# Reciprocal denominators by way of device memory and DMA broadcast, in place of selector products on TensorE

## The reference

```
q = elu(t @ wq.T + bq) + 1 ;  k = elu(t @ wk.T + bk) + 1 ;  v = t @ wv.T + bv      # t: layer-normed tokens
q_cos, q_sin = q * cos, q * sin ; k_cos, k_sin = k * cos, k * sin                  # by token position
kv_cos, kv_sin = sum over tokens of k_cos (x) v, k_sin (x) v                       # 32 x 32 per head
qkv   = q_cos @ kv_cos + q_sin @ kv_sin
denom = 1 / (q_cos . sum(k_cos) + q_sin . sum(k_sin) + 1e-5)                       # one number per token and head
out   = (qkv * denom) joined over heads @ dense_w.T + dense_b                      # added to the stream
```

## Time and profile before

| | us |
|---|---|
| median of 3 runs | 2821.83 |
| the runs | 2802.16, 2821.9, 2821.83 |
| span of the profiled execution, first to last instruction | 2819.6 |
| TensorE / VectorE / ScalarE / GpSimd busy in it | 2421.4 / 2342.6 / 1724.8 / 1866.9 |

### The profile page before, as it was taken

One profiled execution on the slowest core, in us unless ns is written; L12 is line 12 of the kernel. 1 busy time (PEld: TensorE's weight loads), 2 busy tenths in 40 slices (PEclk: granted clock), 3 DMA queues, 4 the chain that ended last, 5 costly groups with the idle time before them and its releaser, 6 DMA issues.

```text
span 2819.6 us, 56945 instructions
## 1 busy us (share of the span) xinstructions
PE 2421.4 (86%) x19300; PEld 1207.1 (43%) x19300; DVE 2342.6 (83%) x3041; ACT 1724.8 (61%) x2821; POOL 1866.9 (66%) x1479
## 2 busy tenths in 40 slices
PE   3379999898989999898999989899998989999872
PEld 3324444444444444444444444444444444444442
DVE  4457999898988889898898989888898988899873
ACT  0057766666666666666666666666666666666640
POOL 0124677777767667776776777676677767777677
PEclk7579999999999999999999999999999999999995
DMA  9100000000000000000000000000000100000000
GB/s 249 35 10 10 10 16 16 16 6 12 16 17 16 16 16 11 7 16 17 16 16 16 14 4 16 17 16 16 17 15 2 16 17 16 16 10 7 7 7 12
DMA packets 232233, 55.14 MB, mean 20 GB/s; under 512 B 226065, under 2 KB 226945, under 8 KB 231777
## 3 DMA queue, kind: packets, MB, share of 16 engines
q1 hardware_dynamic: 231904, 50.95, 9.1%
HBM read 31.19 MB, written 12.85 MB: 16 GB/s over the span
## 4 chain that ended last, share of the span: by engine, by line
PE 40%; DVE 22%; POOL 17%; issue 14%; ACT 3%; DMA 1%; SPq 1%; POOLq 0%; DVEq 0%; ACTq 0%
PE ps L585 10%; PE ps L576 5%; PE ps L610 5%; DVE kbuf L994 5%; POOL prod L844 5%; DVE qbuf L1000 5%; PE ps L627 4%; PE ps L636 3%; POOL prod L847 3%; DVE rs L1017 2%; DVE route L1064 2%; POOL rstd L793 2%; PE ps L601 2%; ACT ebuf L716 2%; PE ps L568 2%
## 5 line engine op out<-in xcount | busy, mean ns | idle before, releaser
L716 ACT ACTIVATE ebuf<-ps,small 112x1024 f32<-112x1024 f32 x448 | 498.6, 1113 | 384.7 <-PE ps L576 357.3
L994 DVE SCALAR_TENSOR_TENSOR kbuf<-ps,ebuf 112x1024 f32<-112x1024 f32 x448 | 546.8, 1221 | 129.4 <-ACT ebuf L716 112.0
L721 ACT ACTIVATE ebuf<-ps,small 128x896 f32<-128x896 f32 x448 | 450.1, 1005 | 317.7 <-PE ps L601 237.8
L815 POOL TENSOR_TENSOR qbuf<-spread_r,qbuf 128x896 f32<-128x896 f32 x224 | 468.2, 2090 | 141.0 <-ACT spread_r L751 140.8
L585 PE MATMUL ps<-kbuf,xcs 112*64 112x512 f32 x1792 | 506.3, 651 | 45.1 <-DVE kbuf L994 45.1
L1000 DVE SCALAR_TENSOR_TENSOR qbuf<-ps,ebuf 128x896 f32<-128x896 f32 x448 | 486.3, 1085 | 37.6 <-ACT ebuf L721 35.3
L793 POOL TENSOR_TENSOR rstd<-varr,power 112x28 f32<-112x28 f32 x64 | 307.2, 4801 | 292.7 <-DVE varr L984 290.7
L636 PE MATMUL ps<-qbuf,gmat 128*64 128x224 f32 x3584 | 403.2, 369 | 4.5 <-DVE pbuf L1028 1.7
L844 POOL TENSOR_TENSOR prod<-prod 112x512 f32<-112x512 f32 x224 | 285.3, 1274 | 159.0 <-DVE prod L1084 157.9
L1084 DVE TENSOR_TENSOR prod<-ps,gate 112x1024 f32<-112x1024 f32 x224 | 272.4, 1217 | 94.4 <-PE ps L661 79.9
L627 PE MATMUL ps<-rs,sel 128*128 128x448 f16 x896 | 249.4, 360 | 96.6 <-issue 81.7
(11 more groups left out here) (133 smaller groups left out, 3668.4 us busy)
## 6 DMA issues: line engine op xcount, KB each, us to landing
qbuf<-in_x SPq DMA_DIRECT2D x8, 1568.0 KB, 12.0
xt<-in_x SPq DMA_DIRECT2D x128, 98.0 KB
out<-ffn SPq DMA_DIRECT2D x128, 98.0 KB
shifted<-nat SPq DMA_DIRECT2D x128, 52.6 KB, 5.0
qbuf<-in_sel SPq DMA_DIRECT2D x1, 1024.0 KB, 11.9
tabn<-in_tabnc SPq DMA_DIRECT2D x1, 784.0 KB, 13.6
p<-in_p2c SPq DMA_DIRECT2D x1, 528.0 KB, 10.4
tabd<-in_tabdc SPq DMA_DIRECT2D x1, 448.0 KB, 11.2
```

Source lines behind the costliest of these rows:

```text
L716: act.activation(ebuf[0:PT, 0, :].rearrange("p (a b) -> p a b", a=2), o[0:PT, :, :], ACT.Exp, bias=minus_one[0:PT, :]).then_inc(kexp_made, 1)
L721: act.activation(ebuf[:, 1, 0:2 * G * PT].rearrange("p (a b) -> p a b", a=2), o[:, :, 0:G * PT], ACT.Exp, bias=minus_one).then_inc(qexp_ma ...
L815: nc.gpsimd.tensor_tensor(qbuf[:, 2:4, n, :], spread_r[:, :, :], qbuf[:, 2:4, n, :], ALU.mult)\
L994: v.scalar_tensor_tensor(kbuf[:, n % 2, :].rearrange("p (a b) -> p a b", a=2), o[0:PT, :, :], 1.0, ebuf[0:PT, 0, :].rearrange("p (a b) -> ...
```

## The change

The reciprocals of a half image (4 or 3 tiles, 16 heads) are stored from `den` to a buffer `r_rows` in device memory, with two DMAs. For each tile, R and RP are each two DMAs issued by SyncE, which read four heads' rows of 448 numbers and write each row to 32 partitions: R into `spread_a` (one buffer), RP into `spread_r` (now two buffers). VectorE and GpSimd multiply `qbuf` by these. The selector products, the 16-bit high and low parts, the ScalarE copies of them and the step RL are gone, with the 1 MiB table of selectors. R and RP leave the PSUM ring.

The step G is one step an image in place of two: TensorE puts all four channel groups in one bank, VectorE writes the whole of `dmat` by one product of the key sums with a 0/1 table (a part of `dsum_sb`), and ScalarE copies `gmat` once.

All times of `schedule()` and all shifts are new, so the order of all steps on all engines differs. The stretch written out before and after the loop is one image longer on either side.

```diff
-    dsum = dsum.astype(np.float32)
+    heads = np.kron(np.eye(HEADS).reshape(CH, HPC, 1, HEADS).transpose(1, 0, 2, 3), np.ones((32, 1, 2, 1)))
+    dsum = np.concatenate([dsum, heads.reshape(128, -1)], 1).astype(np.float32)
...
+    def at_from(self, per, off, base):
+
+        if self.t is None:
+            return self.at(per, off)
+        return (self.t + base) * (2 * per) + (self.c * per + off - 2 * per * base)
...
-RING = ("K", "R", "RP", "Q", "G", "LG", "F", "XC", "ZT", "ZU")
+RING = ("K", "Q", "G", "LG", "F", "XC", "ZT", "ZU")
...
+    add("PL1", [-39.48])
+    add("XT", [-26.05, -25.03])
+    add("SM1", [-17.60])
+    add("CV", [-17.14, -14.85])
+    add("XC", [-14.41])
+    add("XH1", [-10.32])
+    add("CS", [-9.43, -8.38])
+    add("ZT", [-9.01, -2.23])
+    add("K", [-8.08, -5.44, -4.69, -4.23, -2.16, -0.85, -0.56, -0.23, 0.70, 1.75, 2.16, 2.97, 3.48, 4.40])
+    add("KX", [-4.99, -4.00, -2.04, -2.03, -0.59, -0.29, 0.90, 1.81, 2.37, 2.87, 3.14, 4.31, 4.75, 5.40])
+    add("Q", [0.58, 1.89, 2.64, 3.00, 3.96, 4.67, 5.17, 6.33, 6.74, 7.40, 8.98, 9.50, 10.27, 12.75])
+    add("G", [5.99])
+    add("DN", [7.44, 7.51, 8.53, 8.76, 13.92, 13.96, 14.01, 14.20])
+    add("SU", [9.10, 14.95])
+    add("KT", [9.35])
+    add("PN1", [10.11])
+    add("RC", [10.18, 16.12])
+    add("R", [10.94, 12.56, 13.24, 14.41, 16.63, 18.36, 20.21])
+    add("TB", [12.75])
+    add("NM", [13.53, 15.78, 17.73, 18.59, 19.60, 20.70, 23.73])
+    add("RP", [14.50, 15.83, 16.75, 19.54, 20.31, 21.43, 22.52])
+    add("PL2", [17.29])
+    add("T2", [18.91, 19.07, 21.35, 24.06])
+    add("S2", [20.14, 24.13, 24.36, 25.32])
+    add("PN2", [23.08])
+    add("XH2", [28.33])
+    add("SM2", [28.98])
+    add("ZU", [29.03, 29.12])
+    add("RT", [30.90, 31.65, 31.79, 31.89, 32.20, 32.49, 33.08])
+    add("LG", [31.18])
+    add("F", [34.71, 34.94, 35.38, 36.35, 38.26, 39.19, 40.61])
+    add("GT", [37.54])
+    add("OUT", [50.62])
...
+    "vector": {"CV": -0.53, "DN": -0.41, "F": -0.06, "G": -0.07, "K": -0.01, "LG": -0.03, "NM": -0.26, "R": 0.70,
+               "RC": -1.03, "RL": 0.33, "RT": 0.57, "S2": 1.10, "SM1": 4.37, "SM2": -2.37, "XT": -0.14},
+    "scalar": {"G": 1.29, "K": 0.95, "KT": -3.09, "Q": 0.92, "RC": 0.95, "RP": 0.44, "RT": 2.31, "S2": 1.96,
+               "SU": 0.83, "T2": 0.75, "TB": -1.05, "XC": 1.10, "XH1": 0.91, "XH2": 0.75, "XT": 1.17, "ZT": 0.67,
+               "ZU": 1.61},
+    "gpsimd": {"CS": 2.90, "F": 0.79, "GT": -3.31, "OUT": -5.14, "PL1": 30.34, "PL2": 9.78, "PN1": -22.94,
+               "PN2": 3.61, "RP": -2.46, "T2": 0.93},
+    "sync": {"CV": -2.59, "OUT": -3.26, "R": -0.74, "RC": -1.08, "RP": -3.92, "XT": -3.43},
 }
 
-LOOP_FIRST, LOOP_LAST = 3, B - 4
+LOOP_FIRST, LOOP_LAST = 4, B - 5
...
-        r_high = sb("r_high", [128, HALFW], F16)
-        rs = sb("rs", [128, 2, HW4], F16)
...
-        spread_r = sb("spread_r", [128, 2, HW4])
+        spread_r = sb("spread_r", [128, 2, 2, HW4])
+        spread_a = sb("spread_a", [128, 2, HW4])
+        r_rows = nc.dram_tensor("r_rows", [2, HEADS, TILES * HW4], F32).ap()
...
+                if kind == "RC":
+                    w = HALF[n]
+                    rows = r_rows[m.par].rearrange("h (j c t) -> c j h t", j=TILES, c=2)[:, 4 * n:4 * n + w]
+                    sp.wait_ge(recip_made, m.at(2, n + 1))
+                    for c in range(2):
+                        sp.dma_start(rows[c], den[64 * c:64 * c + 16 * w, 0:HALFW]).then_inc(r_stored, 16)
+                if kind == "R":
+                    sp.wait_ge(r_stored, m.at(64, 32 * (n // 4) + 32))
+                    wait(sp, qr_made, m.at_from(7, n, 20 + 7 * m.par + n))
+                    for k in range(2):
+                        heads = r_rows[m.par, 4 * k:4 * k + 4, HW4 * n:HW4 * (n + 1)]
+                        sp.dma_start(spread_a[:, k, :], heads.unsqueeze(1).to_broadcast([4, 32, HW4]))\
+                            .then_inc(a_spread, 16)
+                if kind == "RP":
+                    sp.wait_ge(r_stored, m.at(64, 32 * (n // 4) + 32))
+                    wait(sp, qp_made, m.at_from(7, n - 1, 7 * m.par + n + 1))
+                    for k in range(2):
+                        heads = r_rows[m.par, 8 + 4 * k:12 + 4 * k, HW4 * n:HW4 * (n + 1)]
+                        sp.dma_start(spread_r[:, (7 * m.c + n) % 2, k, :],
+                                     heads.unsqueeze(1).to_broadcast([4, 32, HW4])).then_inc(r_spread[(7 * m.c + n) % 2], 16)
...
-                elif kind in ("R", "RP"):
-                    j, k0 = n, 2 if kind == "RP" else 0
-                    pe.wait_ge(r_made, m.at(2, 1 + j // 4))
-                    pe.wait_ge(r_rows_made, m.at(2, 1 + j // 4))
-                    for k in range(2):
-                        a = 4 * (k0 + k) + j % 4
-                        mm = pe.matmul(o[:, k, 0:HW4], sel16[:, 128 * a:128 * a + 128], rs[:, j // 4, :],
-                                       start=True, stop=True)
-                    mm.then_inc(ring_full, 1)
                 elif kind == "NM":
+                    if n == 0:
+                        pe.wait_ge(g_made, m.at(1, 1))
...
-                    act.wait_ge(ring_full, no + 1)
-                    src = o[:, :, 0:66].rearrange("p k (a o) -> p k a o", a=2)
-                    act.activation(gmat[:, m.par, 2 * n:2 * n + 2, :, :], src[:, :, :, 0:C], ACT.Copy)
-                    for h in range(HPC):
-                        q = slice(32 * h, 32 * h + 32)
-                        for k in range(2):
-                            c = 2 * n + k
-                            last = act.activation(dmat[q, m.par, c, :, HPC * c + h], src[q, k, :, C], ACT.Copy)
-                    last.then_inc(g_made, 1)
+                    act.wait_ge(dmat_made, m.at(1, 1))
+                    act.activation(gmat[:, m.par, :, :, :].rearrange("p c a o -> p (c a) o"),
+                                   o[:, 0, 0:264].rearrange("p (k o) -> p k o", o=33)[:, :, 0:C], ACT.Copy)\
+                        .then_inc(g_made, 1)
                 elif kind == "SU":
                     act.wait_ge(misc_full, no + 1)
-                    wait(act, r_made, m.at(2, n))
+                    wait(act, r_stored, m.at(64, 32 * n))
                     act.activation(den[:, 0:HALFW], o[:, 0:HALFW], ACT.Identity, bias=den_eps).then_inc(den_made, 1)
-                elif kind == "RC":
-                    act.wait_ge(recip_made, m.at(2, n + 1))
-                    wait(act, qr_made, m.at(7, -3 if n == 0 else 0))
-                    act.activation(r_high[:, :], den[:, 0:HALFW], ACT.Copy).then_inc(rhigh_made, 1)
-                    for c in range(2):
-                        last = act.activation(rs[0:64, n, HALFW * c:HALFW * (c + 1)], den[64 * c:64 * c + 64, 0:HALFW],
-                                              ACT.Copy)
-                    last.then_inc(r_rows_made, 1)
-                elif kind == "RP":
-                    act.wait_ge(ring_full, no + 1)
-                    wait(act, qp_made, m.at(7, n))
-                    act.activation(spread_r[:, :, :], o[:, :, 0:HW4], ACT.Copy).then_inc(r_copied, 1)
...
-                    pool.wait_ge(r_copied, m.at(7, n + 1))
-                    nc.gpsimd.tensor_tensor(qbuf[:, 2:4, n, :], spread_r[:, :, :], qbuf[:, 2:4, n, :], ALU.mult)\
+                    slot = (7 * m.c + n) % 2
+                    t0 = 0 if m.t is None else m.t
+                    pool.wait_ge(r_spread[slot], t0 * 224 + 32 * ((7 * m.c + n) // 2 + 1))
+                    nc.gpsimd.tensor_tensor(qbuf[:, 2:4, n, :], spread_r[:, slot, :, :], qbuf[:, 2:4, n, :], ALU.mult)\
...
+                elif kind == "G":
+                    dve.wait_ge(ring_full, no + 1)
+                    ksum = o[:, 0, 0:264].rearrange("p (k o) -> p k o", o=33)[:, :, C:C + 1].to_broadcast([128, 8, HEADS])
+                    v.tensor_tensor(dmat[:, m.par, :, :, :].rearrange("p c a h -> p (c a) h"), ksum,
+                                    dsum_sb[:, 64:].rearrange("p (k h) -> p k h", k=2 * CH), ALU.mult)\
+                        .then_inc(dmat_made, 1)
...
-                elif kind == "RL":
-                    dve.wait_ge(rhigh_made, m.at(2, n + 1))
-                    for c in range(2):
-                        q = slice(64 * c, 64 * c + 64)
-                        last = v.tensor_tensor(rs[64:128, n, HALFW * c:HALFW * (c + 1)], den[q, 0:HALFW], r_high[q, :],
-                                               ALU.subtract)
-                    last.then_inc(r_made, 1)
                 elif kind == "R":
-                    dve.wait_ge(ring_full, no + 1)
-                    v.tensor_tensor(qbuf[:, 0:2, n, :], o[:, :, 0:HW4], qbuf[:, 0:2, n, :], ALU.mult)\
+                    dve.wait_ge(a_spread, m.at(224, 32 * n + 32))
+                    v.tensor_tensor(qbuf[:, 0:2, n, :], spread_a[:, :, :], qbuf[:, 0:2, n, :], ALU.mult)\
```

77 lines of the change are left out of this document (17 added, 60 removed).

## The result

The changed kernel takes 3195.1 us (median of 4 runs, 3186.01 to 3198.11) against 2816.86 us for the kernel before, measured beside it (4 runs, 2802.16 to 2821.9): 1.133 times as long, 95% interval 1.129 to 1.137. Forecast were 2965 us with a range of 2715 to 3300. The direction and the place of the loss were right, the size was not: 378 us more (3195.1 - 2816.9), where 143 were expected (2965 - 2821.8).

A forecast was written before the change was run, and what follows sets the result against it. TensorE and VectorE were both close to full, neither alone the bound; four-engine transfers would lengthen an image from 81.9 to 86.5 us. 2819.6 + 32 x 4.6 - 5 = 2962, with runs about 2 above: 2965 us, range 2715 to 3300.

The forecast's parts named there:

- The transfers: Broadcasts for R and RP: four outer rows mean four of sixteen DMA engines carry 14 pairs, 67 us of every 82.
- The price of a pair: Two broadcasts of one half of a tile's heads on four DMA engines: 75 ns a packet, 4.8 us a pair.
- The waits of R: VectorE idles before R1, R2, R3 and R5 for late transfers; over 10 us an image should name a DMA.
- The work: VectorE's own steps between one R and the next, from 4.5 to 18.2 us, set against the transfers there.
- the part on what is moved: VectorE's work an image, 72.5 - 4.4 + 0.3 + 4.2 = 72.6 us, with 0.6 us for each of seven R meeting GpSimd.
- The slower of each: Each stretch between R steps lasts as long as its transfers or work, whichever is slower: 83.9 us an image, plus 2.6.
- (a): Rival: all sixteen engines carry a broadcast, a pair takes 1.7 us, 78.6 us an image, 2711 us; chance 0.24.
- The store: Writing the next image's reciprocals before the first pair can be fetched: 2.8 us, two issues and a landing of 2.1.
- TensorE's busy time down by 250 us: Sign to look for in the profile after: TensorE loses 28 selector products an image, 249.4 us in all.
- (b): Rival: four engines at their best rate, 4.1 us a pair, 79.5 to 82 us an image, 2740 to 2820 us; chance 0.12.
- (c): Rival: four engines at the loaded rate, 6.3 us a pair, some 3550 us; chance 0.08 including what lies towards the forecast.
- (d): Rival: transfers quick, but each R meets a GpSimd chain, 2.9 us each of seven, 3225 us; chance 0.04.

The follow-up runs named there:

- experiment 1: Changed kernel with each row of reciprocals stored four times, so a broadcast reads 16 outer rows in place of 4: 2773.16 us, 0.981 of the kernel before.
- experiment 2: Changed kernel with rows stored once in the order tile, head: stores led by 64 or 48 rows, broadcasts still by four: 3099.15 us, ratio 1.099.
- experiment 6: Changed kernel with each row stored twice, so a broadcast reads 8 outer rows and writes each to 16 partitions: 2811.55 us, ratio 0.997.
- experiment 5: Changed kernel with rows stored four times (16 outer rows a broadcast), two buffers for R and one for RP: 2720.6 us, ratio 0.965.
- experiment 12: As experiment 2 (four outer rows, order tile, head), with two buffers each for R and RP and gate in a plane of route: 3102.0 us, 1.100.
- experiment 11: As experiment 5, with GpSimd's RP product on one of its two channel groups, heads 12 to 15 left unscaled: 2681.55 us, ratio 0.952.
- experiments 8: Changed kernel with RP reading sixteen outer rows and R four, from a once-stored buffer of its own with further store DMAs: 3160.06 us, ratio 1.120.
- experiment 10: As experiment 1, with the times and shifts of the kernel before and SyncE's new steps set: 3333.09 us, ratio 1.183.
- experiments 7: Changed kernel with rows stored four times, RP reading sixteen outer rows and R four, the first of the copies: 3196.86 us, ratio 1.134.

## Why the direction was right and the size was not

**The transfers.** Four engines carry a broadcast with four outer rows: right. It shows in the DMA share of 0.26, and experiment 1 shows that it decides. The trace has 4-byte packets as well, and their number changes as if each transfer had one for each engine that carries it: from 10577 in the kernel after by 1600 in experiment 2 (64 stores from 4 engines to 16 and 64 from 3), and by 3584 more in experiment 6 (896 broadcasts from 4 engines to 8) or 10752 more in experiment 1 (from 4 to 16). The Trainium skill (DMA: Bandwidth & Descriptors, "Why a DMA increments its semaphore by 16 and not by 1") states the rule that the slowest dimension of both sides sets this number; trace and runs agree. The price of a pair was right too: forecast 75 ns a packet and 4.8 us, and by the packets one takes 74 ns (median) and a pair with nothing but broadcasts beside it 4.7 us (median of 222, from first to last packet). Beside other transfers it takes longer (median 5.6), so that an image's pairs fill 74 us and not 67.

**The waits of R.** The differences between transfers and work in the seven stretches add up to 15.9 us an image; the ten turns show 13.8, the whole run 491.5 / 32 = 15.4. The sum is right, its parts are not, so part of that is luck. Here are the stretches from one R to the next, in us, forecast against the mean of 20 images from 842.8 us on (length and waits from the timeline of VectorE, work from the busy time between two R; the idle time at the end of a stretch that is put down to R's transfer is its wait):

| stretch | forecast work | forecast length | length | work | wait of R | other idle |
|---|---|---|---|---|---|---|
| R0 to R1 | 7.1 | 9.6 | 9.8 | 6.2 | 3.5 | 0.0 |
| R1 to R2 | 4.5 | 9.6 | 10.4 | 4.3 | 1.2 | 4.9 |
| R2 to R3 | 6.3 | 9.6 | 12.2 | 6.3 | 3.3 | 2.6 |
| R3 to R4 | 11.3 | 11.3 | 12.6 | 10.6 | 1.3 | 0.8 |
| R4 to R5 | 10.3 | 14.4 | 13.4 | 12.6 | 0.5 | 0.3 |
| R5 to R6 | 10.3 | 10.3 | 13.4 | 11.0 | 0.3 | 2.2 |
| R6 to R0 | 18.2 | 19.1 | 21.3 | 17.2 | 3.8 | 0.2 |
| an image | 68.0 | 83.9 | 93.1 | 68.4 | 13.8 | 10.9 |

**The work.** The sum took 68.0 us in the stretches, and 68.4 were measured. The 72.6 us of the part on what is moved never entered the sum: its 4.2 us for R's meetings with GpSimd are not in the stretches. They were too high for this kernel. R grew by 267.1 - 242.4 = 24.7 us in all, 0.8 us an image (an R that waits for a late transfer seems to meet GpSimd less often). The routing comparison of the earlier trace rows, L1064 before and L1059 after, fell from a median of 3327 ns to 1366, but the routing steps together grew by 33 us in all (280.1 to 313.2). Where transfers are quick the estimate is nearer: R grew by 336.1 - 242.4 = 93.7 us in experiment 1, 2.9 an image.

**The step that failed: "The slower of each", plus 2.6 us.** I let the waits of R stand in the place of VectorE's other idle time, and kept 2.6 us of it for the lock (VectorE held up by GpSimd) and the loop turn. Over an image as a whole nothing was swallowed. By the windows VectorE had 9.7 us an image of other idle time before, and has 10.9 after; over all fourteen kernels of the table it lies between 9.2 and 12.3 us, while R's waits go from 0 to 23.9 and the period from 75.9 to 100.9. Forecast: 68.0 + 15.9 + 2.6 = 86.5. Measured: 68.4 + 13.8 + 10.9 = 93.1. The 8.3 us of this term, less 2.1 of R's waits, plus 0.4 of work, are the miss of 6.6 us an image (93.1 - 86.5), or 211 us for 32 images. The number stood in my own text, as the 9.4 us that rival (a) gave up only in part, and the forecast left it out.

The stretches show where. From R1 to R2 the slower of each did hold nearly: 4.9 us of other idle time lay inside the transfers, and the length is 10.4 for a forecast of 9.6. From R2 to R3 and from R5 to R6 it was added: 12.2 us for a forecast of 9.6, with 2.6 of other idle time, and 13.4 for 10.3, with 2.2. In experiment 5, where R hardly waits, the stretches from R1 to R2 and from R5 to R6 have 3.5 and 3.2 us of other idle time as well, so most of it there is not made by the transfers. Which steps wait did change from before to after: before it was the experts' product for TensorE and the keys for ScalarE (61.3 and 48.2 us in the ten turns), now keys for ScalarE, queries at the loop's turn, denominators for TensorE (54.8, 49.5 and 46.6). Engines with a fixed order that wait for each other stop together when one stops, and find the same gaps when they go on. That explanation is argued; the sum is shown.

**Inside and outside of the even stretch.** The ten turns grew by 224 us (1638.5 to 1862.2), forecast were 92; what lies outside of them grew by 150 us (2819.6 - 1638.5 against 3193.4 - 1862.2), where 12 images at 4.6 less 5 are 50. At the 11.2 us an image that the turns show it would be 134. R waits longest for its transfers there (8.8 us once); what else makes up the 150 us is open. The store cost more than its 2.8 us, and experiment 2 shows 96 us for its rows.

**TensorE's busy time down by 250 us: wrong.** It has 249.4 us less to do and is busy 24 us longer. The profile gives a granted clock of 0.86 on average against 0.93 before (1 is the upper of its two levels, 2.4 GHz). It is 1.00 in the 20 us before 1490 us, in which TensorE is busy 19.1 us, and 0.74 in the 20 us behind, in which VectorE waits for transfers and TensorE is busy 15.2 us; the same product of key sums takes 701 ns on average, 651 before (L605, L585 before). Where its waits were short, the clock was back: 0.96 and 68.9 us busy an image in experiment 5, against 0.88 and 74.4 after. So in these runs the clock follows the waits. That it adds much to VectorE's other idle time is unlikely, if untested: experiments 2 and 12 have 10.1 and 9.8 us of it at a clock of 0.89, the kernel before 9.7 at 0.95.

**The rivals.** (a), sixteen engines, is experiment 1: for its transfers the description fits (3.3 us from issue to landing, waits gone), and its 2711 us would have been 2773, for the same reason, 6 us of other idle time where 10.7 stayed. (b) and (c) fall with the packet's 74 ns and the pair's 4.7 us. (d) is false here: R's mean is 1192 ns, where (d) has 1.08 + 2.9 us. Half of one GpSimd product is worth 53 us of R in experiment 11.

## What to carry to other kernels

Before a DMA broadcast goes on the path, look at the leading dimension of its source: with four rows four engines carried it, and storing the rows four times over turned 1.133 into 0.981. When waits are put into a pipeline of engines with fixed order, a first estimate adds them to the idle time that is there and doesn't take the larger of the two, unless a trace shows the slack being used, as from R1 to R2 here. Where a transfer feeds one buffer, count the circle of use, issue, transfer and landing beside the load of the engines; if both limits are near each other, taking one away gives little (experiments 8 and 12). An order of work made for one source of the data (experiment 10) may cost 20% with another.

## What the runs showed of the hardware

- Issues on SyncE take longer while the four engines of the broadcasts are full: four issues of the input took 1.88 us in the kernel before, and 7.72 us in experiment 12 at 1462 us.
- A broadcast of 224 KB landed in 3.3 us with sixteen outer rows at a DMA share of 0.42 over the loop, with the queue carrying 104 GB/s; before, a 0.5 KB transfer took 2.1 us. The size costs little over the fixed part once all engines carry it.
- When one transfer runs on four engines beside another on sixteen (experiments 7 and 8), the mean packet is 104 to 110 ns, against 81 with both on four and 95 with both on sixteen, the median 74 in all, and R's transfer was no sooner there (7.46 us after its issue, 7.36 in the kernel after).
- Halving one GpSimd product of 2.1 us took 114.5 us off VectorE's busy time, more than the 52.9 us in R: other VectorE steps were exposed to it too, and 46.3 us are in L982, which has one SBUF input of 112 x 28.
